# Turning five of sixteen feed-forward inputs through VectorE and DRAM instead of TensorE

## The chip, the cores and the metric

The kernel runs on one core of one Trainium2 chip. The metric is the device time of one execution in microseconds (us); a lower number is better. The work is shared by TensorE (PE in the profile, its weight loads PEld), VectorE (DVE), ScalarE (ACT), GpSimd (POOL), and SyncE (SP), which issues the transfers.

## The reference, cut to what matters

The input x has 8 batches of 512 tokens with 128 features. Three blocks follow one another, each with a residual:

```python
x = x + 0.5 * ffn(layernorm(x), W_fc, W_proj)
x = x + attention(layernorm(x))
x = x + 0.5 * ffn(layernorm(x), W_fc, W_proj)

def ffn(x, W_fc, W_proj):
    h = square(relu(x @ W_fc.T))          # 128 -> 512 features
    y = h @ W_proj.T                      # 512 -> 128
    return spikes of 5 steps driven by y, summed, / 5
# attention: keys, values, exp weights, two cumulative sums over the tokens
```

## The kernel before

**Jobs and steps.** There are 16 feed-forward jobs (`FF_JOBS`): jobs 0 to 7 are the first block for batches 0 to 7, jobs 8 to 15 the last block. Job j has lane j % 2 and turn j // 2, and most buffers and semaphores exist once for each lane. The attention of batch b is worked in step `ATT_STEP[b]` (3, 4, 5, 7, 8, 9, 10, 11). All five engines run the same loop over steps `i`, each with its own list of what it does in a step; these lists fix the order by hand. An engine works strictly in that order, so an instruction that waits for a semaphore holds up all that stands behind it on that engine. Step numbers here are values of `i`; "the fold" is `attention_folded`, four small VectorE instructions of step 1 that prepare attention weights.

**The way of one job's input.** VectorE makes the statistics of the four 128-token tiles (`layer_stats`) and from them the mean and variance (`layer_args`: `var_eps`, `neg_mean`). GpSimd raises the variance to -1/2 (`rstd`) and writes the four tiles of `normed` (`normalise`). TensorE turns them from tokens-by-features to features-by-tokens with four matmuls against the identity (`ff_turn`, into the PSUM bank `work`). ScalarE copies the bank rounded to `in_hi` (`ff_hi`), VectorE writes the rest as `in_lo` (`ff_lo`). TensorE then multiplies by W_fc in four chunks of three matmuls each (`ff_expand`); the third matmul of the first chunk waits for `in_lo`:

```python
def product(dst, w_hi, w_lo, x_hi, x_lo, wait_lo=None):
    nc.tensor.matmul(dst, w_lo, x_hi, start=True, stop=False)
    nc.tensor.matmul(dst, w_hi, x_hi, start=False, stop=False)
    if wait_lo:
        pe.wait_ge(*wait_lo)
    return nc.tensor.matmul(dst, w_hi, x_lo, start=False, stop=True)
```

After relu and square on ScalarE, `ff_contract` multiplies by W_proj with four matmuls for each chunk.

**What sets the order around the change.** In step i TensorE turns job i, contracts chunks 2 and 3 of job i-1 (with the turn of the attention input, `att_turn`, between the two, where there is one), expands job i, and contracts its chunks 0 and 1. Two buffers are reused within a lane: `var_eps` and `neg_mean` of job j may be written only when GpSimd has finished `normed` of job j-2 (first line below), and `normed` of job j only when TensorE has turned job j-2 (second line):

```python
dve.wait_ge(normed_made[kind], NT * turn)      # layer_args
pool.wait_ge(turned[kind], turn)               # normalise
```

Of the kernel before, what the change touches and what calls it, by code (L numbers as in the profile page):

```python
# [24 lines left out]
P = 128  # L25
# [15 lines left out]
CONTRACT_ORDER = (0, 1, 2, 3)  # L41

# [8 lines left out]
class FeedForward:  # L51


    def __init__(self, i):
# [5 lines left out]
        self.is_last = i == len(FF_JOBS) - 1  # L60
        if self.is_last:
            self.pool_squares, self.dve_squares, self.act_squares = (LAST_SQUARES[e] for e in ("pool", "dve", "act"))
# [6 lines left out]
def feed_forward(i):  # L69
    return [FeedForward(i)] if 0 <= i < len(FF_JOBS) else []  # L70

# [89 lines left out]
def macaron_kernel(nc, x, wk, bk, wka, bka, wv, bv, gamma, beta, w_fc, w_proj, out):  # L161
# [26 lines left out]
    with ExitStack() as ctx:  # L188
# [54 lines left out]

        in_hi = [sb(f"in_hi{l}", [P, S], F32R) for l in LANES]
# [45 lines left out]
        turned, hi_made, lo_made = sems("turned", KINDS), sems("hi_made", KINDS), sems("lo_made", KINDS)  # L290
        hidden_made, relu_made = sems("hidden_made", LANES), sems("relu_made", LANES)
# [19 lines left out]
        def wait_relu(engine, j, c):  # L311

            engine.wait_ge(relu_made[j.lane], NC * j.turn + c + 1)

# [26 lines left out]
        def _(sp):  # L341
# [9 lines left out]
            for b in range(3, NB):  # L351
                sp.dma_start(x_of["first"][b][:], x_tiles[b]).then_inc(x_loaded[b], 16)
            for b in range(NB - 1):
# [9 lines left out]
        def _(pool):  # L363
# [14 lines left out]
            def normalise(kind, turn, source):  # L378
# [4 lines left out]
                if turn:  # L383
                    pool.wait_ge(turned[kind], turn)
                for t in range(NT):
                    nc.gpsimd.tensor_scalar(normed[kind][:, t, :], source[:, t, :], neg_mean[kind][:, t:t + 1],  # L386
                                            rstd[kind][:, t:t + 1], ALU.add, ALU.mult).then_inc(normed_made[kind], 1)

            def ff_normalise(j):
                if j.index == 0:  # L390
                    first_inverse_deviation(j)
                else:
                    normalise(j.lane, j.turn, x_of[j.layer][j.batch])

            def att_normalise(b):
                normalise("att", b, x_of["att"][b])
# [22 lines left out]
            for i in range(FIRST_STEP, STEPS):  # L419
                for j in feed_forward(i + 2):  # L420
# [11 lines left out]
        def _(act):  # L432
# [13 lines left out]
            def ff_hi(j):  # L446
# [3 lines left out]
                act.wait_ge(turned[j.lane], j.turn + 1)  # L450
# [105 lines left out]
        def _(dve):  # L556
# [67 lines left out]
            def ff_lo(j):  # L624
                if j.index == 0:
# [5 lines left out]
                dve.wait_ge(hi_made[j.lane], j.turn + 1)  # L631
                nc.vector.tensor_tensor(in_lo[j.lane][:], work[j.lane][:], in_hi[j.lane][:].bitcast(F32),  # L632
                                        ALU.subtract).then_inc(lo_made[j.lane], 1)

# [149 lines left out]
            for i in range(FIRST_STEP, STEPS):  # L784
# [3 lines left out]
                for j in feed_forward(i + 1):  # L788
# [61 lines left out]
        def _(pe):  # L850
# [9 lines left out]

# [59 lines left out]
            def ff_contract(j, c):  # L920
                if j.index == 0:
                    pe.wait_ge(proj_ready, 1)
                if j.is_last:
# [4 lines left out]
                    return  # L928
                wait_square(j, c)
# [144 lines left out]
```

## Time and profile before

| | us |
|---|---|
| median of 3 runs | 148.12 (147.59 to 148.47) |
| the profiled execution, its whole time | 147.76 |
| its span in the trace | 146.0 |
| TensorE busy in the span | 140.3 |
| VectorE / ScalarE / GpSimd busy | 117.3 / 113.8 / 95.8 |

The span is what the trace records from the first instruction to the last; 1.8 us lie around it. Busy times overlap, since the engines run side by side. Matmuls are pipelined: one matmul's record is longer than the distance to the next start, so a rate is read from starts.

### The profile page before, as it was taken

Reading aid. Unit: us, or ns where it says so; the run is one execution under the profiler, and the core shown is the slowest. Engines: PE = TensorE matmul, PEld = TensorE weight load, DVE = VectorE, ACT = ScalarE, POOL = GpSimd, SP = SyncE. Lnnn points to the kernel's source line nnn. Section 1 sums busy time; section 2 is a strip of 40 time slices with the busy share of each in tenths; the row PEclk is TensorE's granted clock in tenths of the full one; section 3 lists DMA queues with packets and bytes.
Section 4 is the critical chain, followed back from the end, with each engine's and each line's share of the span. In section 5 each row is a group of like instructions: output and inputs, shape, how many; then the busy total and the mean of one; then the engine's idle time right before and its main releaser. Section 6 shows DMA issues by size and latency. Waiting matters only on the chain.

```text
span 146.0 us, 2901 instructions
## 1 busy us (share of the span) xinstructions
PE 140.3 (96%) x945; PEld 126.1 (86%) x945; DVE 117.3 (80%) x403; ACT 113.8 (78%) x215; POOL 95.8 (66%) x141
## 2 busy tenths in 40 slices
PE   7899999999999999999999999999999999999990
PEld 7689898989989899998988989889789898979790
DVE  3894559388699989999779999999999978453674
ACT  3278877789896996959979697796796977977761
POOL 1439247929999929894998989989967952520300
PEclk9999999999999999999999999999999999999999
DMA  4975000000000000000000000020020102020222
GB/s 140 270 203 161 4 2 0 0 0 4 2 0 2 0 4 2 0 0 0 4 0 0 0 0 7 0 72 0 2 76 0 57 15 72 7 72 0 72 72 72
DMA packets 10510, 5.09 MB, mean 35 GB/s; under 512 B 1152, under 2 KB 10496, under 8 KB 10496
## 3 DMA queue, kind: packets, MB, share of 16 engines
q1 hardware_dynamic: 9808, 4.53, 10.7%
q10 hardware_dynamic: 688, 0.39, 0.9%
q8 instruction: 7, 0.11, 0.3%
q14 instruction: 7, 0.06, 0.1%
HBM read 2.82 MB, written 2.10 MB: 34 GB/s over the span
## 4 chain that ended last, share of the span: by engine, by line
PE 48%; DVE 25%; issue 14%; POOL 6%; DMA 3%; POOLq 1%; ACT 1%; ACTq 1%; DVEq 0%
PE work L932 19%; PE hidden L853 5%; PE hidden L857 5%; PE hidden L854 5%; POOL normed L386 4%; DMA proj_raw<-in_L_ffn_W_proj_dram 3%; DVE weight_sum L699 3%; PE work L866 2%; POOL rstd L380 2%; DVE stats L559 2%; DVE pooled L723 2%; DVE share_bank L713 2%; DVE weight_key L706 2%; DVE share_bank L718 2%; DVE stats_att L559 2%
## 5 line engine op out<-in xcount | busy, mean ns | idle before, releaser
L932 PE MATMUL work<-proj_t,square 128*128 128x128 f32 x480 | 61.2, 275 | 0.0
L932 PEld LDWEIGHTS work<-proj_t,square 128*128 128x128 f32 x480 | 58.8, 192 | 2.4 <-ACT square L460 0.4
L460 ACT ACTIVATE square<-relu 128x512 f32<-128x512 f32 x60 | 37.7, 641 | 0.7
L455 ACT ACTIVATE relu<-hidden 128x512 f32<-128x512 f32 x64 | 36.7, 606 | 0.1
L853 PE MATMUL hidden<-in_hi,fc_lo 128*128 128x512 f32 (+1 forms) x66 | 27.5, 417 | 0.1
L857 PE MATMUL hidden<-in_lo,fc_hi 128*128 128x512 f32 (+1 forms) x66 | 25.6, 387 | 0.0
L854 PE MATMUL hidden<-in_hi,fc_hi 128*128 128x512 f32 (+1 forms) x66 | 25.4, 385 | 0.0
L380 POOL TENSOR_TENSOR rstd<-var_eps,minus_half 128x4 f32<-128x4 f32 x15 | 15.2, 1012 | 14.7 <-DVE neg_mean L572 14.7
L632 DVE TENSOR_TENSOR in_lo<-work,in_hi 128x512 fp32r<-128x512 f32 x15 | 10.2, 680 | 12.3 <-ACT in_hi L451 12.3
L386 POOL TENSOR_SCALAR normed_att<-x_att,neg_mean_att,rstd_att 128x128 f32<-128x128 f32 x32 | 18.1, 578 | 0.8
L386 POOL TENSOR_SCALAR normed<-x_second,neg_mean,rstd 128x128 f32<-128x128 f32 x32 | 16.9, 540 | 0.8
L464 ACT ACTIVATE stairs<-work 128x512 int16<-128x512 f32 (+1 forms) x16 | 9.2, 574 | 7.9 <-PE work L932 6.8
L386 POOL TENSOR_SCALAR normed<-x_first,neg_mean,rstd 128x128 f32<-128x128 f32 x28 | 14.7, 536 | 0.7
L857 PEld LDWEIGHTS hidden<-in_lo,fc_hi 128*128 128x128 f32 x66 | 12.4, 188 | 2.9
L853 PEld LDWEIGHTS hidden<-in_hi,fc_lo 128*128 128x128 f32 x66 | 12.5, 189 | 2.0 <-issue 0.3
L854 PEld LDWEIGHTS hidden<-in_hi,fc_hi 128*128 128x128 f32 x66 | 12.5, 189 | 1.7
L408 POOL TENSOR_TENSOR guess_sum<-weight_sum,guess 128x512 f32<-128x512 f32 x8 | 10.2, 1276 | 5.1 <-ACT guess L509 5.0
L380 POOL TENSOR_TENSOR rstd_att<-var_eps_att,minus_half 128x4 f32<-128x4 f32 x8 | 8.1, 1007 | 8.0 <-DVE neg_mean_att L572 8.0
L451 ACT ACTIVATE in_hi<-work 128x512 fp32r<-128x512 f32 x15 | 8.9, 592 | 4.9 <-PE work L866 4.9
L416 POOL TENSOR_TENSOR guess_share<-weight_key,guess 128x512 f32<-128x512 f32 x8 | 10.2, 1272 | 0.1
L699 DVE TENSOR_TENSOR_SCAN weight_sum<-ones,weight 128x512 f32<-128x512 f32 x8 | 9.7, 1217 | 0.4 <-ACT weight L499 0.4
L723 DVE TENSOR_TENSOR_SCAN pooled<-ones,share_bank 128x512 f32<-128x512 f32 x8 | 9.7, 1210 | 0.0
(118 smaller groups left out, 245.8 us busy)
## 6 DMA issues: line engine op xcount, KB each, us to landing
x_first<-_attn_hidden_states_dram SPq DMA_DIRECT2D x7, 256.0 KB, 4.0
out_dram<-x_out SPq DMA_DIRECT2D x7, 256.0 KB, 2.2
out_dram<-x_out SPq DMA_DIRECT2D x4, 64.0 KB, 1.5
x_first<-_attn_hidden_states_dram ACTq DMA_DIRECT2D x1, 128.0 KB, 2.7
x_first<-_attn_hidden_states_dram SPq DMA_DIRECT2D x1, 128.0 KB, 2.4
fc_raw<-in_L_ffn_W_fc_dram SPq DMA_DIRECT2D x1, 128.0 KB, 2.8
fc_raw<-in_L_ffn_W_fc_dram ACTq DMA_DIRECT2D x1, 128.0 KB, 3.3
proj_raw<-in_L_ffn_W_proj_dram SPq DMA_DIRECT2D x1, 128.0 KB, 3.1
```

What stands on the lines that cost most here:

```text
L380: nc.gpsimd.tensor_tensor(rstd[kind][:], var_eps[kind][:], minus_half[:], ALU.pow).then_inc(rstd_made[kind], 1)
L386: nc.gpsimd.tensor_scalar(normed[kind][:, t, :], source[:, t, :], neg_mean[kind][:, t:t + 1], rstd[kind][:, t:t + 1], ALU.add, ALU.mult).t ...
L408: nc.gpsimd.tensor_tensor(guess_sum[b % 2][:], weight_sum[b % ATT_SETS][:], guess[b % 2][:], ALU.mult).then_inc(guess_sum_made, 1)
L416: nc.gpsimd.tensor_tensor(guess_share[b % 2][:], weight_key[b % 2][:], guess[b % 2][:], ALU.mult).then_inc(guess_share_made, 1)
L455: nc.scalar.activation(relu[j.lane][:, c, :], bank_of_hidden(j, c)[:], ACT.Relu).then_inc(relu_made[j.lane], 1)
L460: nc.scalar.activation(square[j.lane][:, c, :], relu[j.lane][:, c, :], ACT.Square).then_inc(squares_act[j.lane], 1)
L699: nc.vector.tensor_tensor_scan(weight_sum[b % ATT_SETS][:], ones[:], weight[b % ATT_SETS][:], 0.0, ALU.mult, ALU.add).then_inc(sum_made, 1)
L723: nc.vector.tensor_tensor_scan(pooled[:], ones[:], share_bank[:], 0.0, ALU.mult, ALU.subtract).then_inc(pooled_made, 1)
L853: nc.tensor.matmul(dst, w_lo, x_hi, start=True, stop=False)
L854: nc.tensor.matmul(dst, w_hi, x_hi, start=False, stop=False)
L857: return nc.tensor.matmul(dst, w_hi, x_lo, start=False, stop=True)
L932: last = nc.tensor.matmul(work[j.lane][:, tokens], square[j.lane][:, c, tokens], proj_t[:, c, :], start=(c == 0 and t == 0), stop=(c == NC ...
```

## The change

`BLOCK_TURNED` names jobs 3 to 7. TensorE no longer turns them. VectorE transposes `normed` in 32x32 blocks into a new tile `blocks`; SyncE stores it to DRAM, waits, and loads it back with four transfers (one for each 32 partitions) into `block_turned`, with the blocks exchanged; ScalarE and VectorE then make `in_hi` and `in_lo` from `block_turned`, in SBUF, and put the tokens in order as they write. `blocks` and `block_turned` exist three times.

`LAYER_NORM_STEP` says in which step VectorE makes a job's statistics and arguments (GpSimd's part stands one place earlier in its own list, as before). Before, job j had step j-1. Now job 1 and job 2 have step 0, jobs 3 and 4 step 1, jobs 5 and 6 step 2, job 7 step 5; from job 8 on nothing changes. The block transposes stand near the end of the same step as the statistics.

```diff
+LAYER_NORM_STEP = [-1, 0, 0, 1, 1, 2, 2, 5, 7, 8, 9, 10, 11, 12, 13, 14]
+BLOCK_TURNED = [3, 4, 5, 6, 7]
@@ sync
+            for k, index in enumerate(BLOCK_TURNED):
+                j = FeedForward(index)
+                sp.wait_ge(blocks_made[j.lane], blocks_before(j) + 1)
+                sp.dma_start(block_rows[k].ap(), blocks[k % BLOCK_SETS][:]).then_inc(blocks_stored[k], 16)
+                sp.wait_ge(blocks_stored[k], 16)
...
+                for q in range(P // QUARTER):
+                    part = block_turned[k % BLOCK_SETS][q * QUARTER:(q + 1) * QUARTER, :]
+                    sp.dma_start(part.rearrange("p (a n) -> p a n", n=P),
+                                 quarters[q]).then_inc(blocks_loaded[k], 16)
@@ gpsimd
+            def wait_ff_read(j):
+                for last in feed_forward(j.index - 2):
+                    if last.by_blocks:
+                        pool.wait_ge(blocks_made[j.lane], blocks_before(j))
+                    else:
+                        pool.wait_ge(turned[j.lane], turned_before(j))
...
-                for j in feed_forward(i + 2):
+                for j in layer_norms(i + 1):
                     ff_normalise(j)
@@ scalar
+                if j.by_blocks:
+                    k = BLOCK_TURNED.index(j.index)
+                    act.wait_ge(blocks_loaded[k], 16 * (P // QUARTER))
+                    act.wait_ge(hidden_made[j.lane], NC * j.turn)
+                    nc.scalar.activation(in_quarters(in_hi[j.lane]), by_token(block_turned[k % BLOCK_SETS]),
+                                         ACT.Copy).then_inc(hi_made[j.lane], 1)
+                    return
@@ vector
+            def ff_block_turn(j):
+                if j.by_blocks:
+                    dve.wait_ge(normed_made[j.lane], NT * (j.turn + 1))
...
+                    nc.vector.transpose(rows[:].rearrange("p (b t j) -> p t b j", b=P // QUARTER, t=NT),
+                                        normed[j.lane][:].rearrange("p t (b i) -> p t b i", i=QUARTER)
+                                        ).then_inc(blocks_made[j.lane], 1)
...
-                    else:
+                for j in layer_norms(i):
+                    if j.index > 0:
                         ff_layer_stats(j)
-                for j in feed_forward(i + 1):
+                for j in layer_norms(i):
                     if j.index > 0:
                         ff_layer_args(j)
...
+                for j in layer_norms(i):
+                    ff_block_turn(j)
@@ tensor
             def ff_turn(j):
+                if j.by_blocks:
+                    return
```

VectorE's list in steps 1 and 2 is the place where most moves. The number behind a name is the buffer's or the lane's (`normed_0`), for `x_first` the batch's. Before, from `in_lo` of job 1 to `in_lo` of job 2:

```order
L632 TENSOR_TENSOR in_lo1<-work1,in_hi1 128x512 [waits hi_made_1]
L672 TENSOR_TENSOR highest0<-stairs0 128x512 [waits stairs_made_0]
L685 TENSOR_SCALAR count0<-highest0 128x512 [waits highest_made_0]
L762 TENSOR_SCALAR att_w<-att_value,vectors 128x128 [waits beta_mm,fold_mm]
L559 BN_STATS stats_1<-x_first_3 128x6 [waits x_loaded3]
L562 BN_AGGR moments_1<-stats_1 128x2 [waits stats_made_1] x4
L570 TENSOR_REDUCE var_eps_1<-moments_1 128x4 [waits moments_made_1,normed_made_1]
L572 TENSOR_REDUCE neg_mean_1<-moments_1 128x4
L632 TENSOR_TENSOR in_lo0<-work0,in_hi0 128x512 [waits hi_made_0]
```

Of the change, from the arguments of job 4 (ahead of `in_lo` of job 1) to `in_lo` of job 2:

```order
L631 TENSOR_REDUCE var_eps_0<-moments_0 128x4 [waits moments_made_0,normed_made_0]
L633 TENSOR_REDUCE neg_mean_0<-moments_0 128x4
L698 TENSOR_TENSOR in_lo1<-work1,in_hi1 128x512 [waits hi_made_1]
L762 TENSOR_SCALAR count0<-highest0 128x512 [waits highest_made_0]
L708 STREAM_TRANSPOSE blocks0<-normed_1 128x4x4x32 [waits normed_made_1]
L708 STREAM_TRANSPOSE blocks1<-normed_0 128x4x4x32 [waits normed_made_0]
L839 TENSOR_SCALAR att_w<-att_value,vectors 128x128 [waits beta_mm,fold_mm]
L620 BN_STATS stats_1<-x_first_5 128x6 [waits x_loaded5]
L620 BN_STATS stats_0<-x_first_6 128x6 [waits x_loaded6]
L631 TENSOR_REDUCE var_eps_0<-moments_0 128x4 [waits moments_made_0,normed_made_0]
L633 TENSOR_REDUCE neg_mean_0<-moments_0 128x4
L698 TENSOR_TENSOR in_lo0<-work0,in_hi0 128x512 [waits hi_made_0]
```

Job 4's arguments now stand ahead of `in_lo` of job 1, and the two transposes and two jobs' statistics (5 and 6) stand ahead of `in_lo` of job 2, where one job's statistics (3) stood.

GpSimd's list from `normed` of job 3 on was, before:

```order
L386 TENSOR_SCALAR normed_1<-x_first_3,neg_mean_1,rstd_1 128x128 [waits turned_1,rstd_made_1]
L380 TENSOR_TENSOR rstd_att<-var_eps_att,minus_half 128x4 [waits ln_args_made_att]
L386 TENSOR_SCALAR normed_att<-x_att_0,neg_mean_att,rstd_att 128x128 [waits rstd_made_att]
L380 TENSOR_TENSOR rstd_0<-var_eps_0,minus_half 128x4 [waits ln_args_made_0]
L386 TENSOR_SCALAR normed_0<-x_first_4,neg_mean_0,rstd_0 128x128 [waits turned_0,rstd_made_0]
```

And of the change, from the same place:

```order
L429 TENSOR_SCALAR normed_1<-x_first_3,neg_mean_1,rstd_1 128x128 [waits turned_1,rstd_made_1]
L424 TENSOR_TENSOR rstd_0<-var_eps_0,minus_half 128x4 [waits ln_args_made_0]
L429 TENSOR_SCALAR normed_0<-x_first_4,neg_mean_0,rstd_0 128x128 [waits turned_0,rstd_made_0]
L424 TENSOR_TENSOR rstd_1<-var_eps_1,minus_half 128x4 [waits ln_args_made_1]
L429 TENSOR_SCALAR normed_1<-x_first_5,neg_mean_1,rstd_1 128x128 [waits blocks_made_1,rstd_made_1]
L429 TENSOR_SCALAR normed_0<-x_first_6,neg_mean_0,rstd_0 128x128 [waits blocks_made_0,rstd_made_0]
L424 TENSOR_TENSOR rstd_att<-var_eps_att,minus_half 128x4 [waits ln_args_made_att]
L429 TENSOR_SCALAR normed_att<-x_att_0,neg_mean_att,rstd_att 128x128 [waits rstd_made_att]
```

Jobs 4, 5 and 6 now all stand ahead of the first attention input, which came directly behind job 3.

## Rows read from the trace of the kernel before

**Rows 1.** Head of the page, and its section 1.

```profile
span 146.0 us, 2901 instructions
PE 140.3 (96%) x945; PEld 126.1 (86%) x945; DVE 117.3 (80%) x403; ACT 113.8 (78%) x215; POOL 95.8 (66%) x141
```

**Rows 2.** Waits of TensorE: us in total, times, longest.

```profile
PE hidden L993 <- DVE ones L776: 1.0, 1, 1.0
PE share_bank L998 <- DMA fc_raw<-in_L_ffn_W_fc_dram: 0.3, 1, 0.3
PE att_work L963 <- DVE weight_key L706: 0.3, 1, 0.3
PE work L944 <- POOL square L401: 0.2, 1, 0.2
```

**Rows 3.** Chain that ended last, 18 to 32 us: start us, us, what.

```profile
20.39 0.44 PE work L866 x4
...
27.40 0.44 PE work L866 x4
```

**Rows 4.** Timeline of VectorE: start us, us (all of the group), line, operation, idle before.

```profile
9.37 0.15 DVE L572 TENSOR_REDUCE neg_mean<-moments 128x4 f32<-128x4 f32 x1
9.71 0.56 DVE L753 COPY att_t<-att_work 128x384 f32<-128x384 f32 x1 [0.19 <-PE att_work L1021]
...
10.57 0.86 DVE L559 BATCH_NORM_STATS2 stats<-x_first 128x6 f32<-128x128 f32 x4
...
14.10 0.69 DVE L632 TENSOR_TENSOR in_lo<-work,in_hi 128x512 fp32r<-128x512 f32 x1 [2.04 <-ACT in_hi L451]
...
17.22 0.35 DVE L762 TENSOR_SCALAR att_w<-att_value,vectors 128x128 f32<-128x128 f32 x1 [0.15 <-PE att_value L1029]
...
18.54 0.86 DVE L559 BATCH_NORM_STATS2 stats<-x_first 128x6 f32<-128x128 f32 x4
...
22.10 0.71 DVE L693 SCALAR_TENSOR_TENSOR x_att<-count,x_first 128x512 f32<-128x512 uint16 x1
22.85 0.88 DVE L559 BATCH_NORM_STATS2 stats_att<-x_att 128x6 f32<-128x128 f32 x4
...
23.92 0.39 DVE L672 TENSOR_TENSOR highest<-stairs 128x512 int16<-128x512 int16 x1
```

**Rows 5.** Timeline of GpSimd, jobs 1, 2 and 3.

```profile
9.60 1.10 POOL L380 TENSOR_TENSOR rstd<-var_eps,minus_half 128x4 f32<-128x4 f32 x1 [3.75 <-DVE neg_mean L572]
10.80 1.73 POOL L386 TENSOR_SCALAR normed<-x_first,neg_mean,rstd 128x128 f32<-128x128 f32 x4
12.50 1.01 POOL L380 TENSOR_TENSOR rstd<-var_eps,minus_half 128x4 f32<-128x4 f32 x1
13.61 1.73 POOL L386 TENSOR_SCALAR normed<-x_first,neg_mean,rstd 128x128 f32<-128x128 f32 x4
...
21.21 2.26 POOL L386 TENSOR_SCALAR normed<-x_first,neg_mean,rstd 128x128 f32<-128x128 f32 x4
```

**Rows 6.** Timeline of TensorE: turns of jobs 1, 2, attention, and third matmuls.

```profile
12.77 0.60 PE L866 MATMUL work<-ident,normed 128*128 128x128 f32 x4
13.20 1.95 PE L932 MATMUL work<-proj_t,square 128*128 128x128 f32 x16
...
15.46 0.39 PE L857 MATMUL hidden<-in_lo,fc_hi 128*128 128x512 f32 x1
...
20.23 0.60 PE L866 MATMUL work<-ident,normed 128*128 128x128 f32 x4
...
22.92 0.39 PE L857 MATMUL hidden<-in_lo,fc_hi 128*128 128x512 f32 x1
...
28.57 0.60 PE L963 MATMUL att_work<-ident,normed_att 128*128 128x128 f32 x4
```

**Rows 7.** Section 6 of the page: issues, KB each, median us to landing.

```profile
x_first<-_attn_hidden_states_dram SPq DMA_DIRECT2D x7, 256.0 KB, 4.0
out_dram<-x_out SPq DMA_DIRECT2D x7, 256.0 KB, 2.2
```

**Rows 8.** Section 5 of the page: VectorE's cumulative sum, the longest 128x512 operation.

```profile
L699 DVE TENSOR_TENSOR_SCAN weight_sum<-ones,weight 128x512 f32<-128x512 f32 x8 | 9.7, 1217 | 0.4 <-ACT weight L499 0.4
```

**Rows 9.** First matmuls of the kernel, then ScalarE's rounding of job 3.

```profile
1.04 3.35 PE L993 MATMUL hidden<-ones 128*128 128x128 f32 x14 [1.04 <-DVE ones L776]
...
27.95 0.58 ACT L451 ACTIVATE in_hi<-work 128x512 fp32r<-128x512 f32 x1
```

More of the change, by code:

```diff
@@ L70, in feed_forward, with layer_norms @@
     return [FeedForward(i)] if 0 <= i < len(FF_JOBS) else []
+def layer_norms(i):
+    return [FeedForward(k) for k in range(len(FF_JOBS)) if LAYER_NORM_STEP[k] == i]
 def attention(i):
@@ L242, in macaron_kernel @@
         normed = {k: sb(f"normed_{k}", [P, NT, P]) for k in KINDS}
+        blocks = [sb(f"blocks{k}", [P, S]) for k in range(BLOCK_SETS)]
+        block_turned = [sb(f"block_turned{k}", [P, S]) for k in range(BLOCK_SETS)]
+        block_rows = [nc.dram_tensor(f"block_rows{k}", (P, S), F32) for k in range(len(BLOCK_TURNED))]
         in_hi = [sb(f"in_hi{l}", [P, S], F32R) for l in LANES]
@@ L313, in wait_relu, with turned_before, blocks_before, by_token @@
             engine.wait_ge(relu_made[j.lane], NC * j.turn + c + 1)
+        def turned_before(j):
+            return j.before(lambda other: not other.by_blocks)
+        def blocks_before(j):
+            return j.before(lambda other: other.by_blocks)
+        def by_token(tile):
+            return tile[:].rearrange("p (a t j) -> p t a j", a=P // QUARTER, t=NT)
+        def in_quarters(tile):
+            return tile[:].rearrange("p (t a j) -> p t a j", a=P // QUARTER, t=NT)
         def bank_of_hidden(j, c):
@@ L382, in normalise @@
                 pool.wait_ge(rstd_made[kind], turn + 1)
-                if turn:
-                    pool.wait_ge(turned[kind], turn)
+                wait_read()
                 for t in range(NT):
@@ L392, in ff_normalise @@
                 else:
-                    normalise(j.lane, j.turn, x_of[j.layer][j.batch])
+                    normalise(j.lane, j.turn, x_of[j.layer][j.batch], lambda: wait_ff_read(j))
             def att_normalise(b):
-                normalise("att", b, x_of["att"][b])
+                normalise("att", b, x_of["att"][b], lambda: wait_att_read(b))
             def ff_squares(j):
@@ L449, in ff_hi @@
                     return
-                act.wait_ge(turned[j.lane], j.turn + 1)
+                if j.by_blocks:
[5 more added lines that the diff above has]
+                    return
+                act.wait_ge(turned[j.lane], turned_before(j) + 1)
                 nc.scalar.activation(in_hi[j.lane][:], work[j.lane][:], ACT.Copy).then_inc(hi_made[j.lane], 1)
@@ L928, in ff_contract @@
                     return
+                if j.by_blocks and c == 0:
+                    pe.wait_ge(stairs_made[j.lane], STAIRS_A_JOB * j.turn)
                 wait_square(j, c)
```

24 lines of the change are left out of this document (23 added, 1 removed).

## The prediction

> **What bounds the kernel now.** I first read the busy shares: TensorE is busy for 140.3 of 146.0 us, the next engine for 117.3 [rows 1]. Then its waits: beyond the start it waits 0.3 us for VectorE once and 0.2 us for GpSimd once [rows 2]. So TensorE's list of work is the time: what it no longer has to do is won, and what makes it wait is lost in full. Then the chain that ended last, to price a turn on TensorE: 0.44 us for the four matmuls of one job [rows 3]. Last the timelines of VectorE, GpSimd and TensorE through steps 0 to 3, since the change rewrites those two engines' lists there.
>
> **What it removes.** Five turns of 0.44 us on TensorE: 2.2 us [rows 3]. If nothing else moved, the profiled execution would go from 147.76 to 145.6 us.
>
> **What is added off the path.** Five VectorE transposes of 128x512 values. The trace has none. The shortest 128x512 operation near by takes 0.39 us [rows 4], the longest 1.22 us [rows 8]; I take 0.65 us, by `in_lo` with 0.69 us, which moves as many 4-byte values [rows 4]. The Trainium skill, "VectorE: DVE Perf Modes", section "The three transpose paths", gives 311 ns for one 128x128 transpose in bf16; four of them would be an estimate of 1.24 us, about the long end. A round trip through DRAM: a store (2.2 us for 256 KB to DRAM), then four loads of 64 KB (4.0 us to landing for 256 KB) [rows 7]; with four issues one after another I put it at 6 to 9 us. I find job 3 transposed at about 20 us (below), so loaded at 26 to 29; ScalarE rounds job 3 at 27.95 before [rows 9], and after the delays below at about 34.5. Hidden, with 5 us to spare; jobs 4 to 7 have more. SyncE's queue holds nothing else until the first output of the last block, long after. Statistics of jobs 5 and 6 that leave steps 4 and 5 lighten VectorE where TensorE is the bound: no gain.
>
> **What is moved, and what then waits.** Four places, in order of time. The pattern: VectorE works in order, and its list now holds waits for GpSimd ahead of the `in_lo` that TensorE needs.
>
> *A, job 1's turn.* Job 2's statistics now stand ahead of job 1's arguments. Statistics and aggregation of one job take 1.07 us (22.85 to 23.92 [rows 4]). `neg_mean` of job 1 goes from 9.37 to 10.44 [rows 4], and GpSimd's `normed`, which ran from 10.80 to 12.53 [rows 5], ends at 13.60. TensorE's fourth transpose of that turn started at 12.77 + 3 x 0.108 = 13.09 (four take 13.20 - 12.77 [rows 6]). It waits about 0.55 us, a semaphore's passing included.
>
> *B, `in_lo` of job 1.* Job 4's arguments stand ahead of it and wait until GpSimd has normalised job 2, in the same lane. GpSimd takes 2.84 us a job (12.50 + 1.11 + 1.73 [rows 5]), so after job 1 at 13.57 it ends job 2 at 16.4. VectorE gets through the two reductions at 16.65 and ends `in_lo` (0.69 us) at 17.35. TensorE's third matmul stood at 15.46 [rows 6], with A at 16.0. Wait 1.4 us. TensorE is now 1.95 us behind.
>
> *C, `in_lo` of job 2.* The heaviest. The transpose of job 4 stands behind `count` of step 1 and waits for `normed` of job 4, and that waits for TensorE's turn of job 2, which ended at 20.23 + 0.60 = 20.83 [rows 6], now 22.78. So VectorE stands still until 22.8 + 0.05 + 1.73 = 24.6, whatever it has to do. Behind that: transpose 0.65 (25.3), the fold 1.32 (17.22 to 18.54 [rows 4]; 26.6), statistics of jobs 5 and 6, 2 x 1.07 (28.75), four reductions 0.4 (29.15), `in_lo` 0.69: 29.85. TensorE wants it at 22.92 + 1.95 = 24.87 [rows 6]. Wait 5.0 us; with the two bounds of the transpose 4.7 to 5.6. TensorE is 6.95 behind.
>
> *D, the first attention input.* GpSimd gets job 5's arguments at 29.15 and must normalise jobs 5 and 6 before attention 0: 3 x 2.84 = 8.5 us, so 37.7 us. One of the jobs may take longer: `normed` of job 3 took 2.26 us and not 1.73, with VectorE's `x_att`, an operation with two SBUF inputs, running beside it from 22.10 [rows 4, 5]; `x_att` will lie beside job 5 again, so 38.2. Neither number needs the page: the Trainium skill, "GPSIMD Engine Reference", section "Key points", says that GpSimd shares its SBUF interfaces with VectorE and contends with instructions that have two SBUF inputs; by that rule D is 2.8 us, without it 2.3. The trace agrees with it in this one row. TensorE's fourth transpose of the attention turn stood at 28.57 + 0.33 = 28.90 [rows 6]; 6.95 later and one turn (job 3's, 0.44) earlier is 35.4. Wait 2.3 to 2.8 us, I take 2.5. From there on both lists are again in the relation they had; job 7's transpose in step 5 has its `normed` by then, since it takes the place that job 6's layer norm had.
>
> **Sum.** Waits 0.55 + 1.4 + 5.0 + 2.5 = 9.45 us, removed 2.2 us: 7.25 us longer. 147.76 + 7.25 = 155.0 us. The profiled execution lies 0.36 us under the median of 148.12, so I forecast 155.4 us. What a measurement can tell from no change here is about 0.5%, 0.7 us.
>
> **The rivals.**
>
> *Faster: the waits fall into slack and the five turns are won.* It needs the waits A to D to total less than 1.4 us. Its place is C: `in_lo` of job 2 would have to be ready about 2.1 us after TensorE has turned job 2 (22.92 - 20.83 [rows 6]). For it speaks that TensorE alone is the bound [rows 1, 2]. Against it: GpSimd's 1.73 us between that turn and the end of `normed` [rows 5] and the 3.5 us of fold and statistics behind it do not fit into 2.1 us. It would give 145.9 us. Chance 0.05, for an order of waits that I misread.
>
> *D is hidden.* If GpSimd runs two of those jobs while VectorE is still busy, or the statistics are quicker than priced, D falls to 0 and the time is 152.9 us. Against it, GpSimd did not once fall under 2.8 us a job [rows 5]. Chance 0.15.
>
> *The clock.* The kernel's first matmuls, after TensorE had done nothing, took 0.24 us each (14 in 3.35 us [rows 9]), against 0.12 later (16 in 1.95 [rows 6]): that reads as the lower of its two levels. The wait of 5.0 us in C could take it there again. Matmuls at half rate after 29.9 us have a cushion of 2.5 us, as long as D is set by GpSimd; a stretch like that of the start loses 3.35/2 = 1.7 us and would be swallowed. But the wait D itself, after C, could bring a second such stretch that nothing covers: 1.7 to 2.4 us, 157.3 us. The Trainium skill, "TensorE: Matmul & The Clock Gate", section "HAM oscillation", tells of a kernel whose clock falls in every wait for a transfer, and each stretch then starts cold. No row here shows a fall after a wait, since before the change TensorE has none of such length. Chance 0.17.
>
> *The way through DRAM is late.* If one store and four loads took over 14 us, `in_hi` of job 3 would wait; each further us costs one. Rows 7 speak against it. At 16 us it gives 157.4 us. Chance 0.05.
>
> *The forecast itself*: 0.55, own range 154.3 to 156.5 us (the bounds of the transpose and of D). What is left, 0.03, is no change within 0.5%, by a partial slack that I do not see.
>
> **Range and chances.** Down to the hidden D and up to the clock: 152.5 to 157.8 us holds 0.55 + 0.15 + 0.15 and part of the last case. Faster by over 0.5% 0.05, within 0.5% 0.03, slower 0.92.
>
> **What the profile of the changed kernel would show.** In TensorE's waits: a wait of about 5 us for VectorE's `in_lo` at 25 to 30 us, one of about 1.4 us for the same at 16 us, one for GpSimd's `normed` at 13 us and one of 2.5 us for `normed_att` at 35 to 38 us. VectorE idle before a transpose from about 20 to 24.6 us, released by GpSimd. The transposes' duration. Loads landed before 30 us, and ScalarE with no wait on a transfer. From 40 us on each of steps 4 to 7 shorter by 0.44 us. I am wrong if `in_lo` of job 2 is ready before 27 us, if TensorE's matmuls after 30 us take twice their time for long, or if in steps 4 to 7 a new wait for VectorE eats the 0.44 us a step.

## The result: 157.1 us, 6% longer

The changed kernel takes 157.12 us (median of 4 runs, 156.73 to 157.41), the kernel before on the same chip 147.88. The ratio is 1.062 [1.057, 1.067] (a 95% interval stands in brackets here and below): slower. The forecast was 155.4 us; the measured time lies within its range of 152.5 to 157.8, but above the forecast's own range of 154.3 to 156.5. The profiled execution took 157.39 us, 9.63 more than that of before. Four executions of the experiments below were slow ones and are left out of the ratios: two of the kernel with `in_hi` and `in_lo` in the step before (178.9 and 201.1 us, granted clocks of 0.77 and 0.66) and two of 149.1 us of the kernel with jobs 3 and 4 only.

The page of the changed kernel, head, section 1, the granted clock by slices of 3.9 us, the transposes' group and two of the issues:

```profile
span 155.6 us, 2900 instructions
...
PE 142.4 (92%) x925; PEld 125.4 (81%) x925; DVE 121.3 (78%) x408; ACT 115.0 (74%) x215; POOL 97.9 (63%) x141
...
PEclk9999999569999999999999999999999999999999
...
L708 DVE STREAM_TRANSPOSE blocks<-normed 128x512 f32<-128x512 f32 x5 | 3.5, 705 | 8.1 <-POOL normed L429 8.1
...
block_rows<-blocks SPq DMA_DIRECT2D x5, 256.0 KB, 2.0
block_turned<-block_rows SPq DMA_DIRECT2D x20, 64.0 KB, 2.0
```

TensorE's share fell from 96% [rows 1] to 92%, though its list is 20 instructions shorter: the time is now in its waits. The clock has a dent in the eighth and ninth slice that before did not have (the mean over the span was 0.999, now it is 0.978). The transposes took 0.705 us, where the prediction took 0.65, and VectorE stood idle for 8.1 us ahead of them for GpSimd.

TensorE's waits in the changed kernel (us in total, times, longest), against [rows 2]:

```profile
PE hidden L937 <- DVE in_lo L698: 5.9, 2, 4.8
PE hidden L1076 <- DVE ones L853: 1.0, 1, 1.0
PE att_work L1046 <- DVE weight_key L783: 0.8, 2, 0.5
PE hidden L937 <- DVE in_lo L694: 0.5, 1, 0.5
PE att_work L1046 <- POOL normed_att L429: 0.3, 1, 0.3
```

Two waits for `in_lo` of jobs that TensorE still turns (L698) make 5.9 us; the one of 4.8 is C, the other B. The wait for `normed_att`, D, counts only 0.3 us here. Its four turns waited one by one for the four tiles, mostly in their weight loads (1.4 us in four waits there), so its size is read from starts, below. The third and fourth line were not in the forecast.

TensorE's timeline in the changed kernel at the four places, against [rows 6]:

```profile
12.92 0.85 PE L947 MATMUL work<-ident,normed 128*128 128x128 f32 x4
13.61 1.96 PE L1015 MATMUL work<-proj_t,square 128*128 128x128 f32 x16
...
17.13 0.50 PE L937 MATMUL hidden<-in_lo,fc_hi 128*128 128x512 f32 x1 [1.10 <-DVE in_lo L698]
...
29.64 0.80 PE L937 MATMUL hidden<-in_lo,fc_hi 128*128 128x512 f32 x1 [4.79 <-DVE in_lo L698]
...
31.80 0.77 PE L933 MATMUL hidden<-in_hi,fc_lo 128*128 128x512 f32 x1
32.37 0.63 PE L934 MATMUL hidden<-in_hi,fc_hi 128*128 128x512 f32 x1
32.79 0.63 PE L937 MATMUL hidden<-in_lo,fc_hi 128*128 128x512 f32 x1
...
36.78 0.27 PE L1046 MATMUL att_work<-ident,normed_att 128*128 128x128 f32 x1
37.37 1.19 PE L1046 MATMUL att_work<-ident,normed_att 128*128 128x128 f32 x3 [0.32 <-POOL normed_att L429]
38.41 1.06 PE L1015 MATMUL work<-proj_t,square 128*128 128x128 f32 x8
...
55.59 0.66 PE L1046 MATMUL att_work<-ident,normed_att 128*128 128x128 f32 x4 [0.45 <-DVE weight_key L783]
58.13 0.50 PE L937 MATMUL hidden<-in_lo,fc_hi 128*128 128x512 f32 x1 [0.52 <-DVE in_lo L694]
...
81.29 0.60 PE L947 MATMUL work<-ident,normed 128*128 128x128 f32 x4
```

The last of these rows and the first matmul behind D have their counterparts in the trace of before:

```profile
29.00 0.50 PE L932 MATMUL work<-proj_t,square 128*128 128x128 f32 x3
...
71.86 0.60 PE L866 MATMUL work<-ident,normed 128*128 128x128 f32 x4
```

The forecast's sum, taken from starts (each delay is start after minus start before, less what was already there):

| term | forecast | measured | from |
|---|---|---|---|
| A | 0.55 | 0.41 | 13.61 - 13.20 (0.15 of it lie ahead of the turn) |
| B | 1.4 | 1.26 | 17.13 - 15.46 - 0.41 |
| C | 5.0 | 5.05 | 29.64 - 22.92 - 1.67 |
| D, and the clock behind C | 2.5 | 3.13 | 38.41 - 29.00 - 6.72 + 0.44 |
| job 3's turn | -0.44 | -0.44 | |
| four more turns | -1.76 | +0.02 | (81.29 - 38.41) - (71.86 - 29.00) |

The line for D splits at the start of the attention turn: 36.78 - 28.57 - 6.72 + 0.44 = 1.93 us were lost to matmuls that started 0.43 us apart (32.37 to 32.79) and not 0.23, and 1.20 us are the wait for `normed_att`. Up to 38.41 us the forecast had a delay of 9.01 us, measured were 9.41. Behind it, it had 1.76 us coming back, and in sum nothing came. This makes 1.8 of the 2.4 us between the 155.0 us forecast for the profiled execution and its 157.4; 0.4 came before it and 0.2 behind the turn of job 8.

The stretch behind D can be split at the matmuls that follow each attention turn (38.41, 46.56, 56.09 and 73.95 us in the change; 29.00, 37.59, 46.87 and 64.57 before). The last column is an experiment of below, with a short `in_lo`:

| TensorE's time, us | before | the change | if the turns are won | the change, small `in_lo` |
|---|---|---|---|---|
| step 4 | 8.59 | 8.15 | 8.15 | 8.16 |
| step 5 | 9.28 | 9.53 | 8.84 | 9.06 |
| steps 6 and 7 | 17.70 | 17.86 | 16.82 | 17.08 |
| from there to job 8's turn | 7.29 | 7.34 | 7.29 | 7.29 |

So job 4's turn was won. The loss is in steps 5 to 7, and there it can be placed by starts: 0.69 us at the attention turn that waited for `weight_key` (55.59), 0.67 at the wait for `in_lo` of job 6 (58.13), and 0.30 within the attention turn at 73.22.

The chain that ended last, in the changed kernel between 22 and 38 us (start us, us, what):

```profile
22.16 0.45 PE work L947 x4
...
22.77 1.75 POOL normed L429 x4
24.52 4.28 issue
...
28.84 1.01 POOL rstd L424
...
29.96 2.04 POOL normed L429 x4
32.00 1.01 POOL rstd L424
...
33.11 1.75 POOL normed L429 x4
34.86 0.98 POOL rstd_att L424
...
35.93 2.25 POOL normed_att L429 x4
```

TensorE is on it at the start only. Job 4's `normed` waits for the turn of job 2; then GpSimd "issues", which here means that it waits for VectorE to transpose, fold and make the statistics of jobs 5 and 6; then it works with no gap over 0.15 us to 38.18 us, where 37.7 to 38.2 was forecast.

### The profile page after: what moved, and what is told of

Read it like the earlier page. It is cut to its first block, busy times and chain, and to the rows that moved or that the text cites. A ratio compares the mean times of both kernels' runs of the same rounds, so it can differ in the third digit from the quotient of the medians.

```text
span 155.6 us, 2900 instructions
## 1 busy us (share of the span) xinstructions
PE 142.4 (92%) x925; PEld 125.4 (81%) x925; DVE 121.3 (78%) x408; ACT 115.0 (74%) x215; POOL 97.9 (63%) x141
## 4 chain that ended last, share of the span: by engine, by line
POOL 30%; DVE 26%; issue 25%; PE 12%; DMA 2%; ACT 1%; POOLq 1%; ACTq 0%; DVEq 0%
POOL normed L429 12%; POOL normed_att L429 6%; POOL rstd L424 5%; PE work L1015 3%; POOL guess_share L470 3%; DVE stats L620 3%; DVE weight_sum L776 3%; POOL rstd_att L424 3%; DMA fc_raw<-in_L_ffn_W_fc_dram 2%; POOL guess_sum L462 2%; DVE pooled L800 2%; DVE att_lo L714 2%; DVE share_bank L790 2%; DVE in_lo L698 2%; DVE share_bank L795 2%
## 5 line engine op out<-in xcount | busy, mean ns | idle before, releaser
L937 PE MATMUL hidden<-in_lo,fc_hi 128*128 128x512 f32 (+1 forms) x66 | 26.7, 405 | 6.4 <-DVE in_lo L698 5.9
L933 PE MATMUL hidden<-in_hi,fc_lo 128*128 128x512 f32 (+1 forms) x66 | 28.3, 428 | 0.3 <-DVE in_lo L681 0.3
L934 PE MATMUL hidden<-in_hi,fc_hi 128*128 128x512 f32 (+1 forms) x66 | 25.9, 393 | 0.0
L424 POOL TENSOR_TENSOR rstd<-var_eps,minus_half 128x4 f32<-128x4 f32 x15 | 15.6, 1042 | 14.9 <-DVE neg_mean L633 14.9
L429 POOL TENSOR_SCALAR normed_att<-x_att,neg_mean_att,rstd_att 128x128 f32<-128x128 f32 x32 | 18.8, 598 | 0.8
L429 POOL TENSOR_SCALAR normed<-x_second,neg_mean,rstd 128x128 f32<-128x128 f32 x32 | 18.4, 587 | 0.8
L429 POOL TENSOR_SCALAR normed<-x_first,neg_mean,rstd 128x128 f32<-128x128 f32 x28 | 13.3, 489 | 3.4 <-PE work L947 2.7
L470 POOL TENSOR_TENSOR guess_share<-weight_key,guess 128x512 f32<-128x512 f32 x8 | 11.2, 1394 | 0.1
L551 ACT ACTIVATE att_hi<-att_work 128x512 fp32r<-128x512 f32 x8 | 4.8, 598 | 8.3 <-PE att_work L1046 8.3
L698 DVE TENSOR_TENSOR in_lo<-work,in_hi 128x512 fp32r<-128x512 f32 x10 | 6.8, 679 | 5.1 <-ACT in_hi L512 5.1
L708 DVE STREAM_TRANSPOSE blocks<-normed 128x512 f32<-128x512 f32 x5 | 3.5, 705 | 8.1 <-POOL normed L429 8.1
```

The lines of the kernel that those rows point to most:

```text
L424: nc.gpsimd.tensor_tensor(rstd[kind][:], var_eps[kind][:], minus_half[:], ALU.pow).then_inc(rstd_made[kind], 1)
L470: nc.gpsimd.tensor_tensor(guess_share[b % 2][:], weight_key[b % 2][:], guess[b % 2][:], ALU.mult).then_inc(guess_share_made, 1)
```

## The experiments

The first four ask which part costs what.

**One tile of four, in the kernel before.** What five turns are worth on TensorE when nothing is added.

```diff
-                for t in range(NT):
+                for t in (range(NT - 1, NT) if 3 <= j.index <= 7 else range(NT)):
```

> The kernel before, where TensorE makes only the last of the four transposes for jobs 3 to 7 (their input is wrong in three of four tiles; nothing else changes). It takes 5 x 3 x 0.11 = 1.6 us of work from TensorE and leaves every wait as it was. If TensorE alone is the bound through steps 3 to 7: 147.9 - 1.6 = 146.3 us, ratio 0.989. Rival, that VectorE or ScalarE binds there as well and the turns are worth little: over 147.3 us.

Measured: 146.8 us, ratio 0.9935 [0.990, 0.997]: 1.0 us won of 1.63, between the two expectations. From the turn of job 2 to that of job 8 TensorE took 71.97 - 21.56 = 50.41 us, before 51.63. Step 6 gave nothing (55.20 to 63.23, before 54.86 to 62.80); there VectorE had no idle time between two `in_lo`, which fits a step that VectorE bounds as well. In the other four each step got shorter by about 0.33 us, the price of three turns. So 0.44 us a turn is TensorE's price, but not in every step.

**The old steps of the layer norms, all else as in the change.** Job 1's arguments no longer behind job 2's, and only one layer norm a step from step 2 on.

```diff
-LAYER_NORM_STEP = [-1, 0, 0, 1, 1, 2, 2, 5, 7, 8, 9, 10, 11, 12, 13, 14]
+LAYER_NORM_STEP = [-1, 0, 1, 1, 2, 3, 4, 5, 7, 8, 9, 10, 11, 12, 13, 14]
```

> The change with its table of steps alone redone: one layer norm a step, each block-turned job two steps ahead of its use (job 2 back in step 1, jobs 3 to 7 in steps 1 to 5). Theory, that the loss comes from the waits that the table puts ahead of in_lo: no wait of TensorE over 0.7 us, the five turns are won (2.2 us), and at most the 1.8 us of small waits in steps 5 to 7 are lost: 145.9 to 147.7 us, I say 147.2. Rival, that the transposes and the way through DRAM cost by themselves: over 150 us.

Measured: 148.14 us, ratio 1.002 [0.999, 1.005]. The 6% lie in the table of steps. But with all waits of steps 0 to 3 gone, the five turns win nothing either: the stretch from job 2's turn to job 8's is 51.96 us, 1.55 more than with one tile of four. TensorE now waits 1.3 us for `weight_key` and 0.4 us for `in_lo` of a block job. The expectation of 147.2 us (145.9 to 147.7) missed as the prediction did, by the same term.

**The DRAM way made longer.** Every block tile is stored twice before it is loaded.

```diff
                 sp.wait_ge(blocks_stored[k], 16)
+                sp.dma_start(block_rows[k].ap(), blocks[k % BLOCK_SETS][:]).then_inc(blocks_stored[k], 16)
+                sp.wait_ge(blocks_stored[k], 32)
```

> The change, with each block tile stored to DRAM twice, one store after the other, ahead of the loads: the way through DRAM takes 2 us longer (about 8 and not 6). Theory: hidden, 157.1 us within 0.5. Rival, that the way through DRAM is on the path: 2 us or more longer, over 159 us.

Measured: 156.88 us, ratio 1.061 [1.057, 1.066], as the change. The way through DRAM is hidden, and would be with 2 us more. In the changed kernel it takes about 5.8 us for job 3: the store is issued at 19.84, the last load by 23.6, and a load lands 2.0 us (median) later. ScalarE takes it up only at 35.78.

**TensorE kept busy in wait C.** Twenty matmuls of ones (40 records in the trace, in 4.63 us) ahead of the wait for `in_lo` of job 2, into a bank that is free then.

```diff
                 if wait_lo:
+                    for _ in range(fill):
+                        nc.tensor.matmul(att_work[:, 0:P], ones[:, 0:P], ones[:, 0:P], start=True, stop=True)
                     pe.wait_ge(*wait_lo)
```

> The change, with 20 matmuls of ones (128x128, into a free bank) on TensorE directly ahead of its 5 us wait for in_lo of job 2, so that its clock has no reason to fall; the result is unchanged. Theory of one chain (from TensorE's turn of job 2 over GpSimd, VectorE and GpSimd to the first attention input, on which neither the wait for in_lo nor the half clock lies): the matmuls after the wait take 0.23 and not 0.43 us, TensorE gets to the attention turn 1.9 us earlier and waits 1.9 us longer there: 157.1 us, as the change, within 0.5. Rival, each wait and the clock count by themselves: 155.2 us.

Its TensorE, behind the filling:

```profile
29.71 0.50 PE L939 MATMUL hidden<-in_lo,fc_hi 128*128 128x512 f32 x1 [0.30 <-DVE in_lo L698]
30.04 0.39 PE L933 MATMUL hidden<-in_hi,fc_lo 128*128 128x512 f32 x1
30.27 0.40 PE L934 MATMUL hidden<-in_hi,fc_hi 128*128 128x512 f32 x1
...
36.73 1.76 PE L1048 MATMUL att_work<-ident,normed_att 128*128 128x128 f32 x4 [1.53 <-POOL normed_att L429]
38.28 1.92 PE L1017 MATMUL work<-proj_t,square 128*128 128x128 f32 x8
```

The clock stays up (0.23 us a matmul), and the 1.9 us saved turn into 1.53 us of wait for GpSimd: TensorE is behind D at 38.28 us, where in the change, with its low clock on the way, it was at 38.41. Measured: 156.74 us, ratio 1.062 [1.056, 1.068]. The stretch of low clock behind C costs nothing, as the prediction said. The last row shows something else: now the clock is low behind D (8 matmuls in 1.92 us and not 1.06). That was so in the profiled execution, of 158.31 us and a mean granted clock of 0.989. The other three had 1.000 and took 156.34 to 156.74 us: with the same list the clock fell in one execution and not in three. Those three are the cleanest sign that the chain sets the time, since they had no low clock at all and took as long as the change within 0.5 us.

The next three take one cause of C away each. If waits are a sum, each gives back its part; if they are one chain, only the end of GpSimd's work for attention 0 counts.

**Transposes later.** Each step's block transposes stand behind `in_lo` of the next step.

```diff
+                for j in layer_norms(i - 1):
+                    ff_block_turn(j)
                 for b in attention(i - 2):
...
-                for j in layer_norms(i):
-                    ff_block_turn(j)
                 for b in attention(i):
```

> The change, with the block transposes of a step moved behind in_lo of the next step in VectorE's list. Theory of one chain: in_lo of job 2 then waits only for job 4's normed (24.5 us) and ends at about 25.4; the transposes of jobs 3 and 4 follow, GpSimd ends attention input 0 at about 33.9 and not 38.2: 157.1 - 4.3 = 152.8 us, with a longer wait of TensorE for normed_att (about 3 us). Rival, the waits count one by one: the wait for in_lo falls from 5.0 to 0.8 and the half clock goes, 1.9: 151.0 us.

**Tiles of `normed` of their own for the block jobs**, so that job 4's layer norm need not wait for the turn of job 2.

```diff
+        normed_of = {index: sb(f"normed_of{index}", [P, NT, P]) for index in BLOCK_TURNED}
...
             def wait_ff_read(j):
...
+                if not j.by_blocks and j.turn:
+                    pool.wait_ge(turned[j.lane], turned_before(j))
```

> The change, with a normed tile of its own for each block-turned job, so that GpSimd normalises job 4 without waiting for TensorE's turn of job 2. Theory of one chain: VectorE transposes job 4 at 21.8 and not 24.5 us, in_lo of job 2 ends at 26.8, GpSimd ends attention input 0 at about 35.2 and not 38.2: 154.1 us. Rival, the waits one by one (5.0 falls to 2.1, the half clock of 1.9 goes): 152.3 us. If the reuse of the tile has nothing to do with it: 157.1 us.

**`in_lo` first.** In steps 1 and 2, `in_lo` of the step's job stands ahead of the statistics and arguments.

```diff
+                if i in (1, 2):
+                    ff_lo(FeedForward(i))
                 for j in layer_norms(i):
...
-                    if j.index > 0:
+                    if j.index > 2:
                         ff_lo(j)
```

> The change, with in_lo of jobs 1 and 2 ahead of the statistics and arguments of steps 1 and 2 in VectorE's list. TensorE's wait for in_lo of job 1 (1.3 us) goes and that of job 2 falls from 5.0 to 2.4 us. Theory of one chain: the chain only starts 1.3 us earlier and has 0.6 us of in_lo more or as before ahead of the statistics; GpSimd ends attention input 0 at about 37.3: 156.2 us, and TensorE's wait for normed_att grows to 5 us or so. Rival, the waits one by one: 1.3 + 2.6 + 1.9 less: 151.4 us.

What the three measured, with the change for comparison (us; ends and starts from each trace):

| | C: wait, third matmul | `normed_att` ends | next matmul | from there to job 8's turn | time | ratio |
|---|---|---|---|---|---|---|
| the change | 4.79, 29.64 | 38.18 | 38.41 | 42.88 | 157.12 | 1.062 [1.057, 1.067] |
| transposes later | 0.58, 25.61 | 34.46 | 34.79 | 44.47 | 154.01 | 1.043 [1.038, 1.049] |
| own `normed` | 2.14, 26.75 | 35.03 | 35.25 | 44.14 | 154.96 | 1.049 [1.044, 1.053] |
| `in_lo` first | 2.36, 25.73 | 36.90 | 37.11 | 44.35 | 157.84 | 1.069 [1.063, 1.074] |

The third matmul came 2.9 to 4.0 us earlier in all three, but TensorE was past the attention turn only 1.3 to 3.6 us earlier, in each 0.2 to 0.3 us behind GpSimd's end. So what is taken from C is kept only as far as GpSimd's chain gets shorter, and the rest comes back as D: the waits are one chain. The rival, that the waits count one by one, is out: it expected 151.0, 152.3 and 151.4 us. The chain theory's own times were missed too, by 1.2, 0.9 and 1.6 us. The fifth column shows a part of it: in the profiled executions all three take 1.3 to 1.6 us longer behind D than the change. For the first this overstates it: its profiled execution took 155.07 us at a mean clock of 0.975, the other three 153.84 to 154.15 us at 0.985 to 0.989, and its chain ended at 34.46 us, 0.6 later than expected. In the first of them, TensorE's timeline and then windows (us, busy and count of PE, PEld, DVE, ACT and POOL, granted clock, DMA share, GB/s):

```profile
33.22 1.77 PE L1046 MATMUL att_work<-ident,normed_att 128*128 128x128 f32 x4 [2.13 <-POOL normed_att L429]
34.79 1.92 PE L1015 MATMUL work<-proj_t,square 128*128 128x128 f32 x8
```

```profile
28.00:32.00 4.00, 3.10 (x26) 2.84 (x24) 1.30 (x11) 3.22 (x6) 3.90 (x8) 1.00 0.40 131
32.00:36.00 4.00, 2.78 (x10) 2.03 (x11) 2.25 (x4) 0.72 (x2) 2.36 (x5) 0.64 0.40 131
36.00:40.00 4.00, 4.00 (x13) 3.23 (x12) 2.75 (x14) 2.38 (x5) 1.23 (x2) 0.51 0.40 131
```

The granted clock is 0.64 and then 0.51 behind the wait for `normed_att`. In the kernel with `in_lo` first the clock falls twice (0.66 in 28 to 32 us, 0.70 in 36 to 40), and so it gains nothing though its chain ends 1.3 us earlier. That is the prediction's clock rival, in these kernels and not in the changed one. In the changed one the clock fell only behind C, under the cover of D. The length of the wait alone does not tell whether it falls: with own `normed`, matmuls stayed 0.23 us apart behind C's wait of 2.14 us and were 0.43 apart behind D's of 1.57.

The last five ask why the turns of steps 5 to 7 were not won. The two candidates are the transposes, 0.7 us each on VectorE, and `in_lo` of the block jobs. In the change it reads `block_turned` and `in_hi`, both in SBUF; before, it read `work` in PSUM. Its five instances in the changed kernel (ns: least, median, most), and GpSimd's `guess_share`:

```profile
L694 DVE TENSOR_TENSOR in_lo<-block_turned,in_hi x5: 669/833/1495, 36.4 to 74.6; 128x512 fp32r<-128x512 f32 x5
```

```profile
L470 POOL TENSOR_TENSOR guess_share<-weight_key,guess x8: 1272/1280/1748, 46.8 to 121.4; 128x512 f32<-128x512 f32 x8
```

Before, all 15 `in_lo` took 665 to 693 ns and all 8 `guess_share` 1265 to 1281. Step by step (the changed kernel, VectorE, then GpSimd):

```profile
46.55 0.83 DVE L694 TENSOR_TENSOR in_lo<-block_turned,in_hi 128x512 fp32r<-128x512 f32 x1 [1.26 <-ACT in_hi L508]
...
56.58 1.50 DVE L694 TENSOR_TENSOR in_lo<-block_turned,in_hi 128x512 fp32r<-128x512 f32 x1
```

```profile
46.79 1.75 POOL L470 TENSOR_TENSOR guess_share<-weight_key,guess 128x512 f32<-128x512 f32 x1
...
56.25 1.28 POOL L470 TENSOR_TENSOR guess_share<-weight_key,guess 128x512 f32<-128x512 f32 x1
57.48 1.46 POOL L424 TENSOR_TENSOR rstd<-var_eps,minus_half 128x4 f32<-128x4 f32 x1
```

At 46.55 `in_lo` starts ahead of `guess_share`, which starts into it and takes 1.75 us. (`in_lo` itself took 0.83 us and not 0.67, as GpSimd's `guess_sum` ran until 46.84.) At 56.25 `guess_share` starts first, and `in_lo` takes 1.50 us, ending 0.55 after it. Whoever comes second waits for nearly all that is left of the other. This reaches TensorE: in step 5 VectorE stood idle for 0.56 us until the long `guess_share` ended, with `weight_key` behind that on its list, and the 1.50 us stand directly ahead of the wait at 58.13. The Trainium skill, "SBUF — State Buffer", section "SBUF: two separate sides", states this as a lock: the one of the two engines that starts first keeps the shared ports for its whole instruction, and a VectorE operation with two SBUF inputs takes part. Both pairs of rows agree.

**Small transposes** (on the kernel with the old steps): one block in each quadrant in place of sixteen; the rest of `blocks` is zeroed once.

```diff
-                    nc.vector.transpose(rows[:].rearrange("p (b t j) -> p t b j", b=P // QUARTER, t=NT),
-                                        normed[j.lane][:].rearrange("p t (b i) -> p t b i", i=QUARTER)
+                    dve.wait_ge(blocks_cleared, BLOCK_SETS)
+                    nc.vector.transpose(rows[:, 0:QUARTER],
+                                        normed[j.lane][:, 0, 0:QUARTER]
...
+                    for tile in blocks:
+                        nc.vector.memset(tile[:], 0.0).then_inc(blocks_cleared, 1)
```

> e2 (one layer norm a step) with each of the five VectorE transposes cut to one 32x32 block for each 32 partitions (the input of jobs 3 to 7 is then wrong); it takes 0.6 us of VectorE's time out of each of steps 1 to 5. If it is the transposes' own time on a full VectorE that eats e2's gain (148.1 us against 145.6 worked out): 147.0 us or less, and TensorE's wait of 1.0 us for weight_key goes. If it is rather in_lo, which reads two operands in SBUF beside GpSimd's multiplications: 147.9 us.

Measured: 148.16 us, ratio 1.002 [0.998, 1.006]. No gain, but a flawed test: the three memsets of step 0 took 1.56 us of VectorE, the first transpose started 0.15 us behind job 2's turn and not 1.25 ahead of it, and behind that came a new wait of 0.85 us for `in_lo` at 25.35. The stretch from job 2's turn to job 8's took 52.08 us (base 51.96); without the 0.85 us it would be 51.2, so the transposes' own time may have a share in the loss. That is not shown. What is shown is that `in_lo` (up to 1.48 us) and `guess_share` (up to 1.75) stay long without the full transposes.

**Small `in_lo`** (same base): `in_lo` of the block jobs writes 32 of its 512 columns.

```diff
-                    nc.vector.tensor_tensor(in_quarters(in_lo[j.lane]), by_token(block_turned[BLOCK_TURNED.index(j.index) % BLOCK_SETS]),
-                                            in_quarters(in_hi[j.lane]).bitcast(F32),
+                    nc.vector.tensor_tensor(in_lo[j.lane][:, 0:QUARTER], block_turned[BLOCK_TURNED.index(j.index) % BLOCK_SETS][:, 0:QUARTER],
+                                            in_hi[j.lane][:, 0:QUARTER].bitcast(F32),
```

> e2 with in_lo of jobs 3 to 7 cut to 32 of its 512 columns (their low part is then wrong, the waits are as before). It takes 0.6 us from VectorE a job, as e9 does, and also what in_lo and GpSimd take from each other when both read two operands in SBUF (in_lo up to 1.4 us and not 0.67, guess_share 1.75 and not 1.28). If that contention is the cause: 146.2 us, clearly under e9, and all guess_share take 1.28 us. If only VectorE's load counts: as e9, about 147.

Measured: 146.73 us (expected 146.2), ratio 0.990 [0.985, 0.995], 1.4 us less than its base (on another chip); all `guess_share` at 1.27 to 1.29 us; job 2's turn to job 8's in 50.71 us (base 51.96). Its VectorE and GpSimd at one place:

```profile
47.46 0.92 DVE L694 TENSOR_TENSOR in_lo<-block_turned,in_hi 128x32 fp32r<-128x32 f32 x1
```

```profile
47.05 1.28 POOL L470 TENSOR_TENSOR guess_share<-weight_key,guess 128x512 f32<-128x512 f32 x1
```

This `in_lo` has 32 columns and takes 0.17 us elsewhere. Here it takes 0.92 us and ends at 48.38, just behind GpSimd's 48.33: it was held until then. A short operation is held as well.

**Small `in_lo` in the changed kernel itself**, with its own steps.

> The changed kernel with its own step table, and in_lo of jobs 3 to 7 cut to its first 32 columns (the other 480 keep older values, so the output is not the reference's). The four waits up to 38.4 us stay as they are in every theory, since no such in_lo runs before 36 us. Theory (the 1.8 us that steps 4 to 7 give back come from in_lo with both operands in SBUF, beside GpSimd): TensorE goes from the end of the attention turn's wait (38.41 in the changed kernel) to the turn of job 8 (81.29) in about 41.2 us and not 42.88, the guess_share of GpSimd take 1.28 us each and not up to 1.75, and the time is 157.1 - 1.7 = 155.4 us, ratio to before about 1.051. Rival (VectorE's list in those steps is late for another reason, the wait of its list on ScalarE and on GpSimd): the stretch stays near 42.9 us and the time at 156.8 to 157.2 us, ratio 1.060 to 1.063.

Measured: 155.36 us (155.35 to 155.44), ratio 1.050 [1.044, 1.056], 1.76 us under the change. TensorE passes D at 38.03 and turns job 8 at 79.62: 41.59 us in place of 42.88, where 41.2 was expected. All `guess_share` took 1.26 to 1.30 us. Another 0.38 us come ahead of that: `in_lo` of job 3 had run beside `normed_att` and held it (2.25 us in the change, 1.78 here), so D held a piece of the same cause. C is unchanged (4.79 us), and the rival of 157 us is out. The experiment takes some 0.5 us of plain work off VectorE in each step as well as most of the contention, so the 1.76 us can't be put down to the contention alone.

**`in_hi` and `in_lo` in the step before** (base: old steps), so that the two engines don't meet. On ScalarE `in_hi` of the next step's block job goes ahead of `guess`, on VectorE its `in_lo` behind `weight_sum`.

```diff
@@ scalar
+                for j in feed_forward(i + 1):
+                    if j.by_blocks:
+                        ff_hi(j)
@@ vector
+                for j in feed_forward(i + 1):
+                    if j.by_blocks:
+                        ff_lo(j)
```

> e2 with in_hi of a block-turned job ahead of guess on ScalarE and its in_lo behind the cumulative sum of the step before on VectorE, so that it lies beside GpSimd's one-operand normalising and not beside its multiplications. Nothing is left out. If contention and the late in_lo eat e2's gain: in_lo takes 0.70 us, TensorE no longer waits for it, 147.0 us. If VectorE's load alone does: 148.1 us as e2.

Measured: 151.3 us (150.90 to 151.85), ratio 1.021 [1.015, 1.028], where 147.0 or 148.1 was expected. The contention is gone as expected (`in_lo` 0.69 to 0.79 us, `guess_share` at most 1.29), and the time is worse, because `in_lo` now waits for ScalarE ahead of `weight_key`:

```profile
PE att_work L1053 <- DVE weight_key L787: 3.4, 3, 2.0
```

It is the pattern of the change again: a wait for another engine ahead of what TensorE needs. The longest is 2.0 us, and the expectation had no term for it. In the profiled execution the matmuls behind it were 0.43 us apart as well. So this run can't say what the contention costs.

**Jobs 3 and 4 only, with the old steps from job 5 on.**

```diff
-LAYER_NORM_STEP = [-1, 0, 0, 1, 1, 2, 2, 5, 7, 8, 9, 10, 11, 12, 13, 14]
-BLOCK_TURNED = [3, 4, 5, 6, 7]
+LAYER_NORM_STEP = [-1, 0, 1, 1, 2, 4, 5, 6, 7, 8, 9, 10, 11, 12, 13, 14]
+BLOCK_TURNED = [3, 4]
```

> Only jobs 3 and 4 turned in blocks, their layer norms in steps 1 and 2, all other jobs as in the kernel before. Two turns are won, 0.9 us, where VectorE has idle time and before the small waits of steps 5 to 7 begin: 147.0 us. If e2 loses its gain to VectorE's load in steps 4 to 7, this one is the faster; if not, e2 is.

Measured: 147.65 us (median of all twelve), where 147.0 was expected; ratio 0.9963 [0.993, 0.999]. It is the fastest version that does the whole work, but a gain of 0.2 to 0.5 us on the 147.84 of before can hardly be told from no change. The two engines still met: its two `in_lo` in SBUF took 0.69 and 0.84 us, and one `guess_share` 1.75.

## Why the prediction was right, and what it missed

**Right: the mechanism, and its size up to 38 us.** Work and waits for GpSimd were put ahead of what TensorE needs next. A, B and C came where they were put, within 0.15 us each. GpSimd ended attention 0 at 38.18 us of 37.7 to 38.2. The transposes at 0.705 us, DRAM hidden, ScalarE without a wait on a transfer: as said. The old step table takes the whole loss away.

**Right by a cover: the clock.** It fell in C and the loss (1.93 us) was swallowed by D, as the rival's text said. The matmuls put into the wait confirm it: clock up, time unchanged. The second fall, behind D, did not come in the changed kernel (D was 1.20 us). It came in the profiled executions of four variants whose wait at D was 1.5 to 2.9 us, and their stretch behind D was longer by 1.2 to 1.6 us; in one of the four it was missing from the other three executions. The Trainium skill, "TensorE: Matmul & The Clock Gate", section "HAM oscillation", tells of a kernel whose clock falls in each wait for a transfer. The stretches behind C here and behind D there agree with it, 0.43 us a matmul for 0.23, though the waits here were for other engines and not for a transfer. That 157.1 lies by the rival's 157.3 us is chance: its mechanism did not act. It is luck as well that the stated range holds 157.1 us: its top was put at 157.8 for this rival, and a term that the sum did not have filled the room.

**Wrong: "From there on both lists are again in the relation they had", and with it the full 2.2 us removed.** The turns of jobs 3 and 4 were won. In steps 5 to 7 new delays at `weight_key`, `in_lo` and an attention turn took about 1.7 us, as much as the four turns of steps 4 to 7 had to give (1.76 us). The text named this as a thing that would make it wrong, but gave it no term. It reckoned with VectorE and GpSimd slowing each other for one `normed` of GpSimd beside `x_att`, not for `in_lo`, the operation that the diff itself moves from PSUM to SBUF. With `in_lo` cut to 32 columns the changed kernel takes 155.36 us. How the 1.7 us split between contention, the 0.7 us of a transpose and the plain room that VectorE lacks in step 6 (where one tile of four won nothing either) is not settled; the rows of step 5 and of `in_lo` at 56.58 show that contention has a part.

**Loosely put: the sum of waits.** The numbers added up because each wait was worked out after the one before it. But they can't be taken away one by one. The time up to there is set by one chain, job 2's turn to the end of `normed_att`: 38.18 - 22.61 = 15.6 us. Before, TensorE was past its attention turn 8.2 us after the turn of job 2 (29.00, and 20.83 by [rows 6]).

## What to carry to other kernels

On an engine that works in order, a wait for a third engine must not stand ahead of the operand that the bounding engine needs next; two layer norms a step put two such waits on VectorE's list, and they cost 6.3 us (B and C). Follow the chain to its last link before you promise a gain from removing one wait: here what was taken from C was kept only as far as `normed_att` came earlier. And when a diff moves an operand from PSUM to SBUF, look at what GpSimd runs at that moment; an operation of the same length alone is not the same beside it.

## What the runs showed of the hardware

- VectorE's subtraction of two SBUF operands (128x512, 0.67 us alone) took 1.50 us when GpSimd's multiplication had started first, and GpSimd's took 1.75 and not 1.28 us when VectorE had. Even a subtraction of 32 columns (0.17 us alone) was held to the end of GpSimd's and took 0.92 us.
- The granted clock fell behind a wait of 4.79 us, matmuls 0.43 apart and not 0.23. In profiled executions of five other kernels it was also low behind waits of 1.5 to 2.9 us, but not behind D of 1.20 us in the changed one, not behind a wait of 2.14 us with own `normed`, and in three of four executions of the kernel with matmuls in the wait it did not fall at all.
- A VectorE transpose of 128x512 float32 in 32x32 blocks takes 0.705 us; a store of 256 KB and four loads of 64 KB, one queue, about 5.8 us.
